# Rounding of the last two tiles on DVE instead of POOL, and the last tile's gate and up quarters two in a slot

## The reference

```python
x = x + xattn(layernorm(x), ctx)          # 16 heads of 64, 154 context rows, then @ Wo + bo
xn = layernorm(x)
gate = fp4_linear(xn, w_gate)             # 256 -> 704
y    = fp4_linear(xn, w_up)
h    = silu(gate) * y
x = x + fp4_linear(h, w_down)             # 704 -> 256

def fp4_quant_dequant(x):                 # of both operands of fp4_linear
    xb = x in blocks of 16
    scale = max(max(abs(xb)) / 6.0, 1e-12)
    idx = searchsorted([0.25, 0.75, 1.25, 1.75, 2.5, 3.5, 5.0], abs(xb / scale))
    return [0, 0.5, 1, 1.5, 2, 3, 4, 6][idx] * sign(xb / scale) * scale
```

## Time and profile before

| | us |
|---|---|
| median of 3 executions | 928.67 |
| lowest and highest | 928.22 and 934.6 |
| the profiled execution | 934.21 |
| its span in the trace | 932.4 |
| PE busy | 847.9 (91%) |
| DVE busy | 711.9 (76%) |
| POOL busy | 537.5 (58%) |
| ACT busy | 524.9 (56%) |

### The profile page before, as it was taken

How to read it: one execution, slowest core, us unless ns; L and a number is a source line. 1 busy time by engine, 2 the same in 40 slices (tenths; PEclk the granted TensorE clock), 3 DMA queues, 4 the chain that set the end, 5 groups by cost and what they waited for, 6 DMA issues and landing times.

```text
span 932.4 us, 21438 instructions
## 1 busy us (share of the span) xinstructions
PE 847.9 (91%) x6254; PEld 808.8 (87%) x6254; DVE 711.9 (76%) x2142; ACT 524.9 (56%) x1879; POOL 537.5 (58%) x808
## 2 busy tenths in 40 slices
PE   3787699999999999989999999989999999999974
PEld 3666689999988999989988999989988999999864
DVE  5866788877877888877878888876877888888763
ACT  4454455666655565556655565556655555655521
POOL 2444766666554666665554666664653666666652
PEclk9988999999999999999999999999999999999987
DMA  7101000001010000001010000000100000000000
GB/s 227 41 12 51 7 18 12 24 13 41 14 35 19 13 24 13 23 14 41 13 36 18 13 24 13 23 8 20 40 7 24 11 21 13 17 11 13 7 12 11
DMA packets 19869, 23.13 MB, mean 25 GB/s; under 512 B 2642, under 2 KB 18234, under 8 KB 19770
## 3 DMA queue, kind: packets, MB, share of 16 engines
q1 hardware_dynamic: 19770, 21.94, 7.7%
HBM read 17.74 MB, written 4.19 MB: 24 GB/s over the span
## 4 chain that ended last, share of the span: by engine, by line
PE 63%; DVE 22%; issue 6%; ACT 5%; POOL 3%; DVEq 0%; DMA 0%; POOLq 0%; ACTq 0%; SPq 0%
PE ps_q L941 9%; PE ps_g L1019 9%; PE ps_s L979 8%; PE ps_t L989 6%; PE ps_o L1002 5%; PE ps_o L1004 5%; PE ps_o L1003 5%; DVE pT_lo L642 3%; DVE negmax L784 3%; DVE scales L669 3%; PE ps_m L1029 3%; PE ps_g L904 3%; PE ps_m L1031 2%; PE ps_m L1030 2%; PE ps_m L869 2%
## 5 line engine op out<-in xcount | busy, mean ns | idle before, releaser
L477 POOL TENSOR_TENSOR probs<-probs,rsum 128x308 f32<-128x308 f32 x256 | 180.4, 705 | 269.7 <-DVE rsum L748 269.2
L615 ACT ACTIVATE probs<-ps_s,negmax 128x154 f32<-128x154 f32 x512 | 195.2, 387 | 230.2 <-DVE negmax L784 229.1
L784 DVE TENSOR_REDUCE negmax<-ps_s 128x2 f32<-128x308 f32 x256 | 120.8, 472 | 85.3 <-PE ps_s L979 84.9
L1002 PE MATMUL ps_o<-B_sb,pT_lo 128*128 128x256 f32 x640 | 181.3, 283 | 1.3 <-DVE x_both L837 1.2
L1004 PE MATMUL ps_o<-B_sb,pT_hi 128*128 128x256 f32 x640 | 181.0, 283 | 0.0
L1003 PE MATMUL ps_o<-B_sb,pT_hi 128*128 128x256 f32 x640 | 180.7, 282 | 0.0
L642 DVE TENSOR_TENSOR pT_lo<-ps_t,pT_hi 128x256 fp32r<-128x256 f32 (+1 forms) x256 | 122.7, 479 | 38.4 <-ACT pT_hi L519 38.1
L989 PE MATMUL ps_t<-ident,probs 128*128 128x128 f32 x640 | 114.6, 278 | 30.4 <-DVE pT_lo L642 28.9
L1019 PE MATMUL ps_g<-WGU,xqT_hi 128*128 128x352 f32 x512 | 136.7, 349 | 3.5 <-DVE B_sb L642 1.9
L1002 PEld LDWEIGHTS ps_o<-B_sb,pT_lo 128*128 128x128 f32 x640 | 121.4, 190 | 1.7 <-issue 1.7
L1004 PEld LDWEIGHTS ps_o<-B_sb,pT_hi 128*128 128x128 f32 x640 | 121.8, 190 | 0.0
(11 more groups left out here) (149 smaller groups left out, 2206.3 us busy)
## 6 DMA issues: line engine op xcount, KB each, us to landing
xa<-in_x_dram SPq DMA_DIRECT2D x33, 128.0 KB, 2.2
xr<-in_x_dram SPq DMA_DIRECT2D x32, 128.0 KB, 2.0
out_dram<-y_xn SPq DMA_DIRECT2D x32, 128.0 KB, 1.7
W_sb<-in_L_xattn_Wk_dram SPq DMA_DIRECT2D x4, 512.0 KB, 3.4
W_sb<-in_L_xattn_Wv_dram SPq DMA_DIRECT2D x3, 512.0 KB, 3.6
probs<-in_L_xattn_Wq_dram SPq DMA_DIRECT2D x1, 1024.0 KB, 7.9
Wo_sb<-in_L_xattn_Wo_dram SPq DMA_DIRECT2D x1, 1024.0 KB, 7.8
VT<-in_ctx_dram SPq DMA_DIRECT2D x1, 384.0 KB
```

Of the source, the lines that this page charges most:

```text
L477: pool.tensor_tensor(unit, unit, rsum[:, 2 * u:2 * u + 2].unsqueeze(2) .to_broadcast([P, 2, M]), ALU.mult).then_inc(norm_p, 1)
L615: ins = act.activation(probs[:, h, 0:M], ps_s[k % 2][:, s * M:(s + 1) * M], ACT.Exp, bias=negmax[:, h:h + 1], accum_out=sums[:, h:h + 1])
L784: dve.tensor_reduce(negmax[:, 2 * k:2 * k + 2], ps_s[k % 2][:, 0:UM].rearrange("p (h m) -> p h m", h=2), AX_X, ALU.max, negate=True).then_ ...
L1002: pe.matmul(ps_o[:, 0:C], lo[:, j, :], w[:, 0:C], start=first, stop=False)
```

## The change

Three things change, and only behind the end of tile 31's attention.

- `round_x_on_dve`: x of tile 31 is divided and rounded by DVE in step (16, 0), not by POOL.
- `round_h_on_dve`: h of tiles 30 and 31 is rounded by DVE, in columns 0 to 383 and then 384 to 703, with a new semaphore `hl_v`. PE's first group of transposes waits for the first half alone.
- `quarters`: in the step without `before`, that is for tile 31 alone, the gate and up quarters stand two in a slot: 0 and 1 in slot 2, 2 and 3 in slot 3, and what ACT and DVE do for them moves with them.

```diff
+        def quarters(before, k):
+            if before:
+                return [k - 2] if 2 <= k < Q + 2 else []
+            return {2: [0, 1], 3: [2, 3]}.get(k, [])
+        def round_x_on_dve(e):
+            return isinstance(e, int) and e == TILES - 1
+        def round_h_on_dve(d):
+            return isinstance(d, int) and d >= TILES - 2
...
-                    if down and 1 <= k < 4:
+                    if down and 1 <= k < 4 and not round_h_on_dve(d):
                         quantise_hidden(d, (k - 1,))
...
-                    if before and k == 6:
+                    if before and k == 6 and not round_x_on_dve(e):
...
-                    if before and k == 7:
+                    if before and k == 7 and not round_x_on_dve(e):
                         fp4(xn, xc, xsc[:, :], xq_p, 4 * e + 1, (xq_v, 6 * e + 6))
...
-                    if gate and 3 <= k < Q + 3:
-                        q = k - 3
+                    for q in quarters(before, k - 1) if gate else []:
...
+            def round_fp4(v, c, scale, ready, done, before):
+                b = v.rearrange("p (b k) -> p b k", k=BLOCK)
+                dve.wait_ge(*ready)
+                dve.tensor_tensor(v, v, c, ALU.add).then_inc(done, 1)
+                dve.wait_ge(done, before + 1)
+                dve.tensor_tensor(v, v, c, ALU.subtract).then_inc(done, 1)
+                dve.wait_ge(done, before + 2)
+                dve.tensor_tensor(b, b, scale.unsqueeze(2).to_broadcast(list(b.shape)), ALU.mult).then_inc(done, 1)
...
-                    if gate and 3 <= k < Q + 3:
-                        silu(f, k - 3)
+                    for q in quarters(before, k - 1) if gate else []:
+                        silu(f, q)
                     if own and ahead and k == 2:
                         layer_norm1(t + 3, 1 - par, pair + 2 + par)
-                    if gate and 3 <= k < Q + 3:
-                        hidden(f, k - 3)
+                    for q in quarters(before, k - 1) if gate else []:
+                        hidden(f, q)
...
-                        if gate:
+                        if gate and round_x_on_dve(f):
+                            dve.wait_ge(xq_v, 6 * f + 9)
+                        elif gate:
                             dve.wait_ge(xq_p, 4 * f + 4)
                         power(hn[:, 0:F], hc[:, :], (hq_v, 9 * d + 7), hq_v)
                     if down and k == 1:
                         rounder(hc[:, :], hq_v, 9 * d + 3)
+                        if round_h_on_dve(d):
+                            for i, n in enumerate((slice(0, 3 * P), slice(3 * P, F))):
+                                nb = slice(n.start // BLOCK, n.stop // BLOCK)
+                                round_fp4(hn[:, n], hc[:, n], hsc[:, nb], (hq_v, 9 * d + 9), hl_v, 6 * (d - TILES + 2) + 3 * i)
...
-                        dve.wait_ge(xq_v, 6 * e + 3)
-                        dve.tensor_scalar(xri[:, :], xri[:, :], TIES_DOWN, None, ALU.mult).then_inc(xq_v, 1)
+                        if round_x_on_dve(e):
+                            scaled(xn, xn, xri[:, :], xq_v, 6 * e)
+                        else:
+                            dve.wait_ge(xq_v, 6 * e + 3)
+                            dve.tensor_scalar(xri[:, :], xri[:, :], TIES_DOWN, None, ALU.mult).then_inc(xq_v, 1)
...
-                    if gate and 4 <= k < Q + 4:
-                        q = k - 4
+                    for q in quarters(before, k - 2) if gate else []:
                         dve.wait_ge(h_v, Q * f + q + 1)
                         largest(eh[:, q * QF:(q + 1) * QF], hri[:, q * QB:(q + 1) * QB], hq_v)
...
-                        power(xn, xc, (xq_p, 4 * e + 1), xq_v)
+                        power(xn, xc, (xq_v, 6 * e + 4) if round_x_on_dve(e) else (xq_p, 4 * e + 1), xq_v)
                         rounder(xc, xq_v, 6 * e)
+                        if round_x_on_dve(e):
+                            round_fp4(xn, xc, xsc[:, :], (xq_v, 6 * e + 6), xq_v, 6 * e + 6)
                     if gate and k == 7:
-                        if some(f):
+                        if isinstance(f, int) and round_h_on_dve(f - 1):
+                            dve.wait_ge(hl_v, 6 * (f - TILES + 2))
+                        elif some(f):
...
-                        pe.wait_ge(xq_p, 4 * f + 4)
+                        if round_x_on_dve(f):
+                            pe.wait_ge(xq_v, 6 * f + 9)
+                        else:
+                            pe.wait_ge(xq_p, 4 * f + 4)
                         m_free((y_v, d), (xqT_lo, f + 1))
                         transposes(xn, KT, xqT_mm)
                     if down and k in (4, 5):
                         r = k - 4
-                        if r == 0:
+                        if round_h_on_dve(d):
+                            pe.wait_ge(hl_v, 6 * (d - TILES + 2) + 3 * r + 3)
+                        elif r == 0:
                             pe.wait_ge(hq_p, 3 * d + 3)
                         m_free((xqT_lo, e) if r == 0 else (hqT_lo, 2 * d + 1), (hqT_lo, 2 * d + r + 1))
                         transposes(hn[:, 3 * r * P:3 * (r + 1) * P], 3, hqT_mm)
...
-                    if gate and 2 <= k <= Q + 1:
-                        gate_up(f, k - 2)
+                    for q in quarters(before, k) if gate else []:
+                        gate_up(f, q)
```

More of the change, by code:

```diff
@@ L152, in xattn_ffn_kernel @@
         gu_mm, th_a, silu_v, h_v = (sem(n) for n in ("gu_mm", "th_a", "silu_v", "h_v"))
-        hq_v, hq_p, hqT_mm, hqT_hi, hqT_lo = (sem(n) for n in ("hq_v", "hq_p", "hqT_mm", "hqT_hi", "hqT_lo"))
+        hq_v, hq_p, hl_v, hqT_mm, hqT_hi, hqT_lo = (sem(n) for n in ("hq_v", "hq_p", "hl_v", "hqT_mm", "hqT_hi", "hqT_lo"))
         d_mm, y_a, y_v = sem("d_mm"), sem("y_a"), sem("y_v")
```

## The result

| | before | changed |
|---|---|---|
| median of 8 executions, us | 933.75 | 937.73 |
| lowest and highest, us | 928.22 and 934.6 | 934.59 and 941.12 |
| profiled execution, us | 934.21 | 934.7 |
| its span, us | 932.4 | 932.9 |

What follows compares the result with a forecast made beforehand. The prediction took PE to bound most of the span, with the change acting only at the end. Its stretches, +4.1 +3.7 -3.1 = +4.7 us, moved the median from 928.67 to 933.4 us, range 929.5 to 939.0.

Steps and rivals of the forecast that it cites:

- rival D: Whole execution: runs lie near 928.5 or 934.4; if the median falls on the upper level, 939 to 940 us; chance 10%.
- Stretch 1: Up to tile 31's first gate matmul: `xqT_lo` stands behind six DVE operations, so that matmul comes 4.1 us later.
- Rival C: DVE operations with two full SBUF inputs are much dearer, adding 2.8 us at two places: 940.1 us; chance 4%.
- Stretch 2: From tile 31's first gate matmul to the scaling of its h: 15.69 us for 12.03, +3.7 taken.
- the down product of tile 30: Late in stretch 2, up to the add of y: 2.42 us at full clock, 3.67 mostly at half clock.
- The half clock throughout: Case of stretch 2 with PE at half clock all along: 17.29 us, +5.3, total 935.0 us.
- pause ahead of quarter 2: In stretch 2, PE waits for `hidden` of quarter 0 behind `silu` of quarter 1: a new pause of 1.10 us.
- to the first `hqT_lo`: In stretch 2, from quarter 3's tanh: tanh 0.35 and five short operations at about 0.25, 1.6 us.
- Stretch 3: From the scaling of tile 31's h to the end: second transposes start 5.95 us after it, not 9.09; -3.1 us.
- Rival A: Shorter DVE operations decide at all three places, -7.6 us, 921.1 us; chance 3%.
- Rival B: In stretch 2 the clock stays full, so the kernel is not slower: 928.2 to 929.8 us; chance 8%.
- its own signs: Behind tile 31's attention: gate matmul 4 us later, clock near 0.50 in quarters; wrong if `xqT_lo` within 2 us or clock above 0.8.

Runs made afterwards that it cites:

- four parts: Kernel before with one piece of the change each: x of tile 31, tile 30's h, tile 31's h, paired quarters; ratios 1.0013, 1.0027, 0.9967, 1.0047.
- pairs only: Kernel before with only tile 31's gate and up quarters two to a slot, all rounding on POOL; median 936.29 us, ratio 1.0047.
- tile 31's h only: Kernel before with only h of tile 31 rounded on DVE in halves; median 928.70 us, ratio 0.9967.
- x only: Kernel before with only x of tile 31 rounded on DVE, quarters one to a slot; median 934.09 us, ratio 1.0013.
- tile 30's h only: Kernel before with only h of tile 30 rounded on DVE in halves; median 936.32 us, ratio 1.0027.
- the reordered kernel with dummies: Changed kernel with quarters one to a slot, DVE's list reordered and dummy matmuls in PE's pauses; against before, median 926.07 us, ratio 0.9935.
- the one experiment on it: Kernel before with 12 dummy matmuls ahead of the transposes of the probabilities in the first four steps; median 960.47 us, ratio 1.0297.
- with dummies: Changed kernel with dummy matmuls, whose result nobody reads, in PE's pauses behind tile 31's attention; against before, median 931.31 us, ratio 0.9982.

## Why the prediction was wrong

**The base.** The sum was set on a median of three executions, 928.67, and the predicted 933.4 is below what the kernel before itself takes in eight, 933.75: against that base the number reads as no loss at all. The prediction saw the spread (rival D) and called it two levels near 928.5 and 934.4. That reading failed. The 35 executions of before beside the four parts fill 929.2 to 937.2. Rival D, with 939 to 940 and a chance of 10%, came nearer to the measured 937.73 than the forecast did, which had 72% for 931.5 to 935.5. The range of 929.5 to 939.0 held the measurement only because it had been widened for the half clock and for rival D. Six of the profiles, by the reciprocal of tile 31's x, which no edit can have moved by then, and the granted clock from 20 to 160 us:

| kernel | reciprocal at | granted clock, 20 to 160 us |
|---|---|---|
| changed | 889.76 | 0.96 |
| pairs only | 890.09 | 0.96 |
| tile 31's h only | 893.08 | 0.95 |
| x only | 895.47 | 0.94 |
| before | 895.92 | 0.94 |
| tile 30's h only | 897.97 | 0.91 |

The more of the half clock in the set-up, the later everything behind it. (The other profiles follow this roughly: the reordered kernel with dummies has 0.98 and 890.45.) From 160 to 880 the clock reads 1.00 in all of them. The profile of before, 934.21, was near its median, while that of the changed kernel, 934.7, was one of its fastest executions, and this hides the effect in the two profiled times. That the clock is the cause of the level is not shown. The two go together in the traces, and the one experiment on it missed.

**The difference.** Forecast +4.7, measured +5.8 over the executions and +6.7 in the profiles. By the steps of the prediction:
- *Stretch 1*, +4.1: it is +4.15, with 0.42, 0.48 to 0.49 and 0.56 for the operations on DVE (0.41, 0.48, 0.55 expected). The transposes of x gained nothing, as forecast. Rival C, dearer operations, is out. The granted clock was 0.84 over PE's pause of 5.05 us, and the first gate matmuls behind it took 0.95, for 0.59 at the full clock. The Trainium skill, "TensorE: Matmul & The Clock Gate", section "HAM oscillation", says that a wait between groups of matmuls brings the half clock back. This pause agrees with it; behind the shorter one of 1.99 us the second transposes still ran at the full clock (0.52).
- *Stretch 2*, +3.7 taken, +5.3 kept for the range: it is +5.34. **The term that was mis-sized is the down product of tile 30**: 2.42 us at the full clock was taken, 4.22 at the half clock was measured, 1.80 too little. The step that failed is the choice of the clock. "About the end of quarter 3" it did come back (the first transposes took 0.49 at 909.39, the second 0.52 at 911.87), but it was gone again for the down product, 0.50 from 913.6, behind pauses of 1.99 and 1.26 us. Before, it had lasted 4.2 us with no matmul at all, and I took that for the rule. The half clock throughout, 17.29, came near the measured 17.37 only because it priced this down product too low as well (3.67, from a row in which the clock came back towards the end) and the second transposes too high. All other terms were right within 0.1, and with dummies only those fall whose time goes in long rows of matmuls:

| term of stretch 2, us | forecast | changed | with dummies |
|---|---|---|---|
| quarters 0 and 1, to the tanh of 1 | 3.93 | 3.92 | 2.23 |
| pause ahead of quarter 2 | 1.10 | 0.99 | 0.99 |
| quarters 2 and 3, to the tanh of 3 | 3.93 | 3.84 | 2.23 |
| to the first `hqT_lo` | 1.6 | 1.58 | 1.59 |
| to the second transposes | 0.60 | 0.70 | 0.70 |
| to the down product | 1.81 | 1.78 | 1.78 |
| down product, to the add | 2.42 | 4.22 | 2.41 |
| add to scaling | 0.30 | 0.34 | 0.34 |
| sum | 15.69 | 17.37 | 12.27 |

- *Stretch 3*, -3.1: it is -2.83. The second transposes start 6.00 after the scaling, 5.95 forecast; what follows took 8.69 for 8.43, with the clock at 0.56 in the last down product.
- *Rival A*, that the shorter operations decide, is out: x alone gains nothing (gate +0.91, ratio 1.0013 with an interval on both sides of 1) and tile 30's h alone costs; only where nothing is queued behind it, at tile 31's h, does the shorter rounding pay. The Trainium skill, "GPSIMD Engine Reference", section "4.1 Engine selection", calls GpSimd about twice as slow with two inputs. Here an addition of 704 columns took 1.69 on POOL and 0.56 + 0.48 in two halves on DVE, 1.6 times as long. The section says nothing on the queue.
- *Rival C*, out as said, was also priced too high. POOL's 1.69 for 704 columns is 0.92 for 384 and 0.77 for 320, which is 0.37 and 0.29 above DVE's, not 0.50 and 0.42: +2.0 in stretch 1 and in stretch 3, not +2.8.
- *Rival B*, the full clock: it did not happen by itself in the profiled execution. Made to happen, it gives 36.0 for 36.5 before, the even result that B stood for.

With the right base the same sum would have given 933.75 + 4.7 = 938.5 for the 937.73 measured. That this is so close is partly luck: the medians differ by 4.0 us, the estimate over all executions by 5.8 and the two profiles by 6.7. By its own signs the mechanism was right: `xqT_lo` starts 4.1 us later, and the granted clock in the quarters was 0.58.

## What to carry to other kernels

Before moving work to a faster engine, read what stands behind it in that engine's list: here six short operations ahead of `xqT_lo` cost 3.2 us, and behind it 0.2. Grouping work by two puts everything of the first behind the wait of the second; what used to lie beside matmuls then lies bare, and that was the larger loss. Set a sum on the profile's stretch and compare stretches, since the executions of one kernel here differ by more than the change, and read the clock of each stretch beside it, since that differs between executions too.

## What the runs showed of the hardware

- The same 18 matmuls of a down product took 2.4 us at a granted clock of 1.00 and 4.2 us at 0.50. Filling PE's pauses with dummy matmuls took 7.1 us from the changed kernel and 2.3 us from the last stretch with tile 31's h alone on DVE, with no delay at the first gate matmul (11.07 for 11.08, 6.94 for 6.94).
- The clock is not a fixed property of the code. Up to quarter 0 the kernel with tile 31's h only does what the kernel before does, at the same distances from the reciprocal (gate 6.94 and 6.93), and its quarters 0 and 1 ran at the full clock, where those of before and of pairs only (6.95) ran at the half one:

```profile
900.02 0.59 PE L1054 MATMUL ps_g<-WGU,xqT_hi 128*128 128x352 f32 x2 [1.01 <-DVE xqT_lo L655]
```

- In the same way x only and before have the same last stretch up to the second transposes (9.09), and then 8.98 and 8.43 us to the end. In all three profiles with pairs and without dummies, though, the down product of tile 30 began at the half clock (0.55 for its first matmul).
- Executions of one kernel differ by 8 us of 930. The profiles, with a granted clock of 0.91 to 0.98 from 20 to 160 us, differ by as much at the reciprocal.
- Scales of 44 numbers took 0.50 us with POOL adding and 0.19 with POOL idle, in the changed kernel at 894.30 as in the earlier trace rows. In the kernel before this operation is there 33 times. The 14 that took 0.46 to 0.76 us started inside an addition or subtraction of POOL and ended 0.03 to 0.05 us behind it; the other 19, with POOL idle or within 0.17 us of the end of its operation, took 0.18 to 0.21. So it is not slowed by a factor but held until POOL's operation is over:

```profile
229.89 0.74 POOL L447 TENSOR_TENSOR y_xn<-y_xn,hc 128x256 f32<-128x256 f32 x1
```

```profile
229.93 0.74 DVE L675 TENSOR_SCALAR scales<-scales 128x44 f32<-128x44 f32 x1
```

The Trainium skill, "GPSIMD Engine Reference", section "8. Key points", says that GpSimd shares its SBUF interfaces with VectorE and that some of VectorE's instructions contend with it; these rows agree.
